# Delta-rule attention stage: the output's inverse root taken one step earlier, the second chunk's gate products and q_eps at other steps

## The reference, cut to what matters

```
q = l2norm(q) * scale;  k = l2norm(k)            # 8 heads, dk 96, dv 192
def step(S, inp):
    S = S * exp(g_t)
    delta = (v_t - k_t . S) * b_t
    S = S + k_t (x) delta
    o_t = q_t . S
g_out = (h @ Wg).reshape(B, T, H, dv)
o = rmsnorm(o, onorm_w) * silu(g_out)
x = x + o.reshape(B, T, H * dv) @ Wo
```

## Time and profile before

| | us |
|---|---|
| time of the kernel before, median of 3 runs | 3762.31 |
| lowest and highest of the runs | 3756.7, 3772.59 |
| the profiled execution's own time | 3786.4 |
| its span, first to last instruction | 3784.6 |
| delta stage and what stands ahead of it: 0 to 85 | 85.0 |
| delta stage, 85 to 1631 | 1546.0 |
| all behind it, 1631 to 3784.6 | 2153.6 |
| in the delta stage busy: TensorE matmuls | 1390.39 |
| VectorE | 1139.47 |
| ScalarE | 910.44 |
| GpSimd | 786.37 |
| TensorE's mean granted clock in the delta stage | 0.93 |

### The profile page before, as it was taken

One profiled execution on the slowest core, in us unless ns is written; L12 is line 12 of the kernel. 1 busy time (PEld: TensorE's weight loads), 2 busy tenths in 40 slices (PEclk: granted clock), 3 DMA queues, 4 the chain that ended last, 5 costly groups with the idle time before them and its releaser, 6 DMA issues. The chain is left out here.

```text
span 3784.6 us, 87201 instructions
## 1 busy us (share of the span) xinstructions
PE 3303.1 (87%) x32714; PEld 2481.1 (66%) x32714; DVE 2725.0 (72%) x5753; ACT 2038.9 (54%) x4599; POOL 1798.9 (48%) x1631
## 2 busy tenths in 40 slices
PE   4789999999999999968999999986898699899998
PEld 3577777787777777845666566654666366656665
DVE  5677777777778777557777677775999477767775
ACT  3555666566666556514666366632444366636662
POOL 3355555555555555334665266632121466526662
PEclk8789999999999999989999999997999799999999
DMA  4111111111111111032122321231212222131122
GB/s 124 24 24 25 27 25 27 25 25 25 25 25 25 25 25 24 11 105 71 46 54 52 94 49 46 71 82 49 49 47 55 63 53 65 45 90 44 47 71 70
DMA packets 409630, 182.71 MB, mean 48 GB/s; under 512 B 235808, under 2 KB 384384, under 8 KB 406656
## 3 DMA queue, kind: packets, MB, share of 16 engines
q1 hardware_dynamic: 409216, 177.15, 19.1%
HBM read 94.47 MB, written 40.12 MB: 36 GB/s over the span
## 5 line engine op out<-in xcount | busy, mean ns | idle before, releaser
L1197 POOL TENSOR_TENSOR delta_cv<-delta_cv,delta_last_tap 96x256 f32<-96x256 f32 (+1 forms) x384 | 332.8, 867 | 667.8 <-DVE delta_cv L1626 667.8
L1933 POOL TENSOR_TENSOR g_a_rn<-g_a_clip,g_minus_half 128x16 f32<-128x16 f32 x64 | 186.4, 2912 | 270.9 <-DVE g_a_clip L2197 242.7
L1933 POOL TENSOR_TENSOR f_a_rn<-f_a_clip,f_minus_half 128x16 f32<-128x16 f32 x64 | 186.3, 2912 | 260.5 <-DVE f_a_clip L2197 232.2
L2150 ACT ACTIVATE g_a_pr<-g_ps,g_a_nb,g_a_rn 128x128 f32<-128x128 f32 x512 | 185.9, 468 | 146.4 <-DVE g_a_nb L2231 146.4
L2150 ACT ACTIVATE f_a_pr<-f_ps,f_a_nb,f_a_rn 128x128 f32<-128x128 f32 x512 | 185.9, 468 | 146.3 <-DVE f_a_nb L2231 146.3
L1461 ACT ACTIVATE delta_cv<-delta_ps,delta_conv_qk 96x256 f32<-96x256 f32 x256 | 121.2, 473 | 237.1 <-PE delta_ps L1294 236.2
L1618 DVE SCALAR_TENSOR_TENSOR delta_cv<-delta_ps,delta_conv_qk,delta_cv 96x256 f32<-96x256 f32 x256 | 122.1, 477 | 161.3 <-ACT delta_last_tap L1463 161.0
L1238 PE MATMUL delta_ps<-delta_state,delta_qk 96*128 96x192 f32 x1024 | 198.4, 338 | 17.2 <-issue 12.7
L1618 DVE SCALAR_TENSOR_TENSOR delta_cv<-delta_ps,delta_conv_v,delta_cv 128x256 f32<-128x256 f32 x192 | 92.0, 479 | 152.1 <-ACT delta_last_tap L1463 150.5
L1238 PEld LDWEIGHTS delta_ps<-delta_state,delta_qk 96*128 96x128 f32 x1024 | 168.0, 193 | 31.0 <-issue 27.5
L1461 ACT ACTIVATE delta_cv<-delta_ps,delta_conv_v 128x256 f32<-128x256 f32 x192 | 91.0, 474 | 172.0 <-PE delta_ps L1294 171.9
(11 more groups left out here) (350 smaller groups left out, 10472.1 us busy)
## 6 DMA issues: line engine op xcount, KB each, us to landing
f_a_vm<-f_a_v SPq DMA_DIRECT2D x128, 130.0 KB, 2.3
g_a_vm<-g_a_v SPq DMA_DIRECT2D x128, 130.0 KB, 2.3
delta_gd<-delta_dram_row SPq DMA_DIRECT2D x16, 1024.0 KB, 4.7
window_vm<-window_v SPq DMA_DIRECT2D x64, 128.0 KB, 2.3
f_m_x<-y SPq DMA_DIRECT2D x24, 256.0 KB, 3.5
delta_dram_inv<-delta_sub SPq DMA_DIRECT2D x16, 256.0 KB, 2.1
f_m_more<-x SPq DMA_DIRECT2D x16, 256.0 KB, 3.9
x<-f_m_x SPq DMA_DIRECT2D x16, 256.0 KB, 2.3
```

Of the source, the lines that this page charges most:

```text
L1197: pool.tensor_tensor(cv[0:M, t % 3], cv[0:M, t % 3], last_tap[0:M, t % 3], ALU.add).then_inc(summed.sem, 1)
L1933: pool.tensor_tensor(rn[:, u % 2], clip[:, u % 2], minus_half[:], ALU.pow).then_inc(rn_sb.sem, 1)
L2150: e = act.activation(pr[:, u % 2, half, i, :], ps[:, score_bank(u, half), i * P:(i + 1) * P], ACT.Exp, bias=nb[:, u % 2, half, i:i + 1], s ...
```

## The change

The gate products of odd chunks go from chunk steps 2, 2, 5 to 2, 5, 12, which is step 22, 25 and 4 of the next unit; even chunks keep theirs. For this every use of `GATE_AT`, `OT_AT` and `Y_AT` gets a pair of tables and a helper `chunk_of`; the steps of `ot` and `y` stay. The power goes from chunk step 14 to 13 (unit steps 19 and 5) and to the end of GpSimd's step, so that for even chunks it stands directly behind the last part of the substitution. q_eps goes from chunk step 3 to 6 (unit steps 12 and 26). The load of `ht` follows the last gate product of the unit before and goes from step 3 to 5.

```diff
+    def chunk_of(t, at, cc):
+        C = chunk(t, at)
+        return C if C is not None and C % 2 == cc else None
...
-    GATE_AT, OT_AT, Y_AT = (2, 2, 5), (21, 22, 25), 27
+    GATE_AT, OT_AT, Y_AT = ((2, 2, 5), (2, 5, 12)), ((21, 22, 25), (21, 22, 25)), (27, 27)
     def misc_uses(t):
-        for k, when in enumerate(GATE_AT):
-            C = chunk(t, when)
+        for cc in range(2):
+            for k, when in enumerate(GATE_AT[cc]):
+                C = chunk_of(t, when, cc)
+                if C is not None:
+                    yield "gate", C, k
...
             for t in range(LAST):
-                n = unit(t, 31)
+                n = unit(t, START + GATE_AT[1][2] - HALF + 1)
                 if n is not None and n + 2 < UNITS:
                     take(sp, ("gate", 2 * n - 1, 2))
                     load_ht(n + 2)
...
-                C = chunk(t, 14)
-                if C is not None:
-                    ostat_step.need(pool, C)
-                    o_normed.need(pool, C - 1)
-                    pool.tensor_tensor(of[:], ostat[:, 1, :], minus_half[:, 0:H], ALU.pow).then_inc(of_sb.sem, 1)
...
+                C = chunk(t, 13)
+                if C is not None:
+                    ostat_step.need(pool, C)
+                    o_normed.need(pool, C - 1)
+                    pool.tensor_tensor(of[:], ostat[:, 1, :], minus_half[:, 0:H], ALU.pow).then_inc(of_sb.sem, 1)
...
-                C = chunk(t, 3)
+                C = chunk(t, 6)
                 if C is not None:
                     q_summed.need(dve, C)
                     ostat_step.need(dve, C - 2)
                     dve.tensor_scalar(q_eps[:, C % 2], q_sum[:, C % 2], 1e-6 * DK, 1e-12 * DK, ALU.mult, ALU.add)\
```

More of the change, by code:

```diff
@@ L990, in delta_attention @@
     INVERT_AT = dict(x4=23, y4=25, x5=28, y5=30, x6=32, y6=34)
-    GATE_AT, OT_AT, Y_AT = (2, 2, 5), (21, 22, 25), 27
+    GATE_AT, OT_AT, Y_AT = ((2, 2, 5), (2, 5, 12)), ((21, 22, 25), (21, 22, 25)), (27, 27)
     def misc_uses(t):
-        for k, when in enumerate(GATE_AT):
-            C = chunk(t, when)
-            if C is not None:
-                yield "gate", C, k
-        for k, when in enumerate(OT_AT):
-            C = chunk(t, when)
-            if C is not None:
[L1002 to L1005, removed]
+        for cc in range(2):
[3 more added lines that the diff above has]
+                    yield "gate", C, k
+        for cc in range(2):
+            for k, when in enumerate(OT_AT[cc]):
+                C = chunk_of(t, when, cc)
+                if C is not None:
+                    yield "ot", C, k
+        for cc in range(2):
+            C = chunk_of(t, Y_AT[cc], cc)
+            if C is not None:
+                yield "y", C
         for i in range(2):
@@ L1149, in _ @@
                                     .then_inc(u16_in.sem, 16)
[L1150 to L1154, removed]
+                for cc in range(2):
+                    C = chunk_of(t, Y_AT[cc] + 1, cc)
+                    if C is not None:
+                        copied(sp, ("y", C))
+                        row = C // PER * ROWS + PAD + C % PER * P
+                        sp.dma_start(dst[row:row + P, :], out[:, cc]).then_inc(stored[cc].sem, 16)
             for i in range(2):
@@ L1297, in misc @@
             def misc(t):
-                for k, when in enumerate(GATE_AT):
-                    C = chunk(t, when)
-                    if C is not None:
[L1301 to L1322, removed]
+                for cc in range(2):
+                    for k, when in enumerate(GATE_AT[cc]):
+                        C = chunk_of(t, when, cc)
+                        if C is not None:
+                            bank = claim(pe, ("gate", C, k))
+                            mm = pe.matmul(ps[:, bank, :], ht[:, C // 2 % 3, 3 + cc * P:3 + (cc + 1) * P], wg[:, k * 512:(k + 1) * 512],
+                                           start=True, stop=True)
+                            filled(mm, ("gate", C, k))
@@ new lines, in misc @@
+                for cc in range(2):
+                    for k, when in enumerate(OT_AT[cc]):
+                        C = chunk_of(t, when, cc)
+                        if C is not None:
+                            o_normed.need(pe, C)
+                            bank = claim(pe, ("ot", C, k))
+                            for i in range(4):
+                                m = 4 * k + i
+                                mm = pe.transpose(ps[:, bank, i * P:(i + 1) * P],
+                                                  o[:, cc].rearrange("p h v -> p (h v)")[:, m * P:(m + 1) * P], ident[:])
+                            filled(mm, ("ot", C, k))
@@ L1323, in misc @@
+                for cc in range(2):
+                    C = chunk_of(t, Y_AT[cc], cc)
+                    if C is not None:
+                        copied(pe, ("ot", C, 2))
+                        bank = claim(pe, ("y", C))
+                        for m in range(NV):
+                            mm = pe.matmul(ps[:, bank, 0:D], ot[:, m, :], wo[:, m, :], start=m == 0, stop=m == NV - 1)
+                        filled(mm, ("y", C))
                 for i in range(2):
@@ L1483, in misc @@
             def misc(t):
[L1484 to L1496, removed]
+                for cc in range(2):
+                    for k, when in enumerate(GATE_AT[cc]):
+                        C = chunk_of(t, when, cc)
+                        if C is not None:
+                            o_gated.need(act, C - 1)
+                            bank = take(act, ("gate", C, k))
+                            emptied(act.activation(gate[:, k * 512:(k + 1) * 512], ps[:, bank, :], ACT.Silu), ("gate", C, k))
+                for cc in range(2):
+                    for k, when in enumerate(OT_AT[cc]):
+                        C = chunk_of(t, when, cc)
+                        if C is not None:
+                            take(act, ("y", C - 1))
+                            bank = take(act, ("ot", C, k))
+                            emptied(act.activation(ot[:, 4 * k:4 * k + 4, :], ps[:, bank, :].rearrange("p (m i) -> p m i", i=P), ACT.Copy),
+                                    ("ot", C, k))
                 for m in range(4):
@@ L1629, in misc @@
             def misc(t):
[L1630 to L1635, removed]
+                for cc in range(2):
+                    C = chunk_of(t, Y_AT[cc], cc)
+                    if C is not None:
+                        y_in[cc].need(dve, C // 2)
+                        stored[cc].need(dve, C // 2 - 1)
+                        bank = take(dve, ("y", C))
+                        emptied(dve.tensor_tensor(out[:, cc], ps[:, bank, 0:D], yres[:, cc], ALU.add), ("y", C))
                 for cc in range(2):
```

## The result

The changed kernel takes 3739.46 us (median of 9 runs, 3733.22 to 3749.3) against 3768.7 us of the kernel before (9 runs, 3756.7 to 3785.67): ratio 0.992 with a 95% interval of 0.9905 to 0.9935, so some 30 us faster.

A forecast was written before the change was run, and what follows sets the result against it. TensorE was taken to set the pace. 15 x (1.0 - 2.9) = -28 us on the profiled 3786.4 us gave 3758, scaled to the timed median as 3734 us; own range 3721 to 3757, with rivals 3715 to 3766.

The forecast's parts named there:

- The bound and the chain: Delta stage, steps 19 to 23: TensorE sets the pace and stalls 2.55 us behind GpSimd's products and ScalarE's gate.
- The power, 1.4 us: Even chunks, step 20 to 19: run in GpSimd's idle time, the power lets the gate multiplications end 1.4 us earlier.
- The order of the banks, 0.6 us: Steps 22 to 25: with the second gate product moved, x4 waits for one eviction, 0.6 us a unit gained.
- The product at step 4, +1.0 us: Steps 3 to 6, where TensorE has no room: the third gate product costs 1.0 us a unit, bounds 0.86 and 1.7.
- q_eps and the load, 0: q_eps at steps 12 and 26, load of ht at step 5: no gain or loss; 4 us kept for q_eps's range.
- The clock, in the middle: Steps 22 to 25: between falls as often as now (12.3 us) and never (10.5), 11.4 us taken, a gain of 2.9.
- the case "never": Steps 22 to 25: the clock no longer falls at all, 10.5 us a window; 3720 us in all, chance 0.08.
- The base of the sum: The -28 us were taken from the profiled execution's 3786.4 us, 0.64% above the timed median, then scaled by the ratio.
- The rival of a late substitution: GpSimd ends the substitution late, so the power pushes tile 20 and later tiles: +31 us, 3793 us, chance 0.08.
- the moved stall: Steps 25 to 0: VectorE or the inverse's transfers are late, the gain stays in VectorE's queue: 3762 us, chance 0.12.
- The rival that the clock falls as before: The 1.5 us stall left may be enough for the clock to fall as often: -15 us, 3747 us, chance 0.24.

The follow-up runs named there:

- The filled stall: The kernel before with five products of 240 columns that nobody reads, issued at step 23 ahead of the first vt transposes: ratio 0.9938 to the kernel before.
- the q_eps run: The kernel before with only q_eps moved, from chunk step 3 to 6: ratio 1.0001 to the kernel before.
- the run at 2, 5, 10: The changed kernel with odd chunks' third gate product at chunk step 10 (unit step 2) in place of 12: ratio 0.9883 to the kernel before.

## Why the prediction was right, and where it was not

The forecast ratio was 0.9926 and the measured one is 0.992. Point by point:

- **The bound and the chain** were right: the chain GpSimd, ScalarE, ring, TensorE is what the power alone shortened.
- **The power, 1.4 us:** 1.44 us (12.49 to 11.05 at the full clock).
- **The order of the banks, 0.6 us:** 0.49 us (11.05 to 10.56). Together 1.93, forecast 2.0. The stall left is 1.50 us as forecast.
- **The product at step 4, +1.0 us:** 1.14 us, inside its bounds. In the sum of the windows fewer falls of the clock hide it (6 before, 4 after), which the prediction had not counted.
- **q_eps and the load, 0:** 1.0001 for q_eps. Its median of 171 ns away from GpSimd's long products agrees with the exclusion that the Trainium skill states (SBUF — State Buffer, Who interferes with whom). The load stands in the runs of the gate products and no wait on it shows.
- **The clock, in the middle:** here the size was off. The step that failed is "I take the middle", 11.4 us for steps 22 to 25. It measured 10.60 us, nearly the case "never", for which I had given 0.08. The filled stall shows that the falls hang on the idle time; how much of it is too much was not to be had from the kernel before, and no run here gives such a length.
- **The base of the sum:** I subtracted from the profiled execution, whose clock fell more often than is usual for that kernel. By the two traces the stage became 52 us shorter, up to its last tile; by the medians the kernel became 29 us faster. Against the trace of the q_eps run, which is near the median, steps 22 to 25 gain 3.1 us a unit (13.68 to 10.60), where I had 2.9. The error of the base and the one on the clock went against each other, so it is partly luck that the total is closer than its parts.

I gave the three parts one sum and didn't say that, by my own terms, the gate products' move is a loss (1.0 against 0.6 us). Measured it is 21 us, the power is -48 us, together -27 us; the change as a whole is -30 us. The rival of a late substitution did not come: the power ends as the next tile arrives, with nothing to spare in the unit shown. Nor did the moved stall: steps 25 to 28 sum to the same 135.3 us in both kernels. The rival that the clock falls as before, and with it what the Trainium skill (TensorE: Matmul & The Clock Gate, A second HAM failure mode: psum-queue depth-cycling) would lead one to expect of short waits on the ring, did not come for the changed kernel's waits of 0.16 + 1.50 us (1 window of 15) and came in full where the power was late (15 of 15, waits of 3.06 us in most).

What stays open: why the clock falls in steps 3 to 6 in six windows of one kernel and in one or two of another, and what besides the idle time decides on a fall in steps 22 to 25: the kernel before keeps its clock in two units with the same wait of 2.5 us behind which it falls in others, and the run at 2, 5, 10 has the waits of the changed kernel and 3 windows below 1.00 in place of 1.

## What to carry to other kernels

Cut a change with several moves into its parts: here one part gave 48 us and another took 21 us of it. Work on a shared engine is cheap only where it fits into a wait that it doesn't lengthen: three products cost 0.35 us a unit in steps 15 to 20, one cost 0.76 us in steps 0 to 3, though the engine was idle for 2 us there. And with a ring of two banks the place of the read-out in the other engine's stream counts as much as that of the product. A wait of TensorE is worth its length and what the clock does after it; the second can be as large as the first.

## What the runs showed of the hardware that I had not expected

75 products that nobody reads made the kernel 0.6% faster; TensorE was then granted its full clock (1.00) through all 15 windows from step 22 to 25, in place of 3. A fall of the clock just ahead of a stall cost little: steps 20 to 22 lasted 1 us longer and the wait behind them was 1 us shorter (4.70 and 1.57 us against 3.7 and 2.55). And executions of the same kernel before differed by 19 us in one round, with mean granted clocks of 0.947 to 0.957.
